# Layer 1's node stage: own values and residual added by TensorE, the result taken out by ScalarE

## The reference, cut to what matters

```
q = ((src @ q_w.T + q_b) * scaling).reshape(n, H, HD)
...
ex = jnp.exp(w - mx[e_dst])
den = jax.ops.segment_sum(ex, e_dst, num_segments=n)
attn_w = ex / (den[e_dst] + 1e-16)
msgs = attn_w[:, :, None] * v[e_src]
agg = jax.ops.segment_sum(msgs, e_dst, num_segments=n)
attn_out = agg.reshape(n, D) @ out_w.T + out_b
x = _batchnorm(src + attn_out, g1, b1)
ff = jax.nn.leaky_relu(x @ lin1_w.T + lin1_b, negative_slope=0.01)
ff = ff @ lin2_w.T + lin2_b
x = _batchnorm(x + ff, g2, b2)
```

## Time and profile before

| | |
|---|---|
| median of 3 runs | 5938.26 us (5937.13 to 5941.97) |
| profiled execution | 5949.69 us |
| its span | 5947.6 us |
| busy over the span | PE 70%, DVE 64%, ACT 32%, POOL 68% |
| mean granted TensorE clock | 0.756 |
| node stage, from L2335 to the first product of the feed-forward part | 2352.6 to 2402.7 us |

### The profile page before, as it was taken

The page is one execution under the profiler, slowest core; times in us unless marked ns, Lnnn a source line. Parts: engine busy times, 40 slices in busy tenths (PEclk is TensorE's granted clock), DMA queues, the critical chain, the costliest instruction groups (busy, mean ns, idle before and its releaser), DMA issues. The chain is left out here.

```text
span 5947.6 us, 86128 instructions
## 1 busy us (share of the span) xinstructions
PE 4163.2 (70%) x19030; PEld 3346.8 (56%) x19030; DVE 3780.3 (64%) x11775; ACT 1879.7 (32%) x4142; POOL 4018.2 (68%) x4191
## 2 busy tenths in 40 slices
PE   4788888867777676897788788444444457777776
PEld 4677776746666565444555555333333346666665
DVE  8565555547777777646666666444444447777776
ACT  5132222233343332463333333011111123444443
POOL 2677777757777775006777777677777767777773
PEclk9988778767777876998888888655555557777777
DMA  2554444434444444165554554222222234545442
GB/s 59 132 140 117 120 117 120 119 109 136 140 136 136 140 136 123 59 288 171 157 159 154 161 155 153 65 64 68 63 69 64 69 111 137 151 144 149 147 147 78
DMA packets 426775, 738.45 MB, mean 124 GB/s; under 512 B 100522, under 2 KB 280579, under 8 KB 419700
## 3 DMA queue, kind: packets, MB, share of 16 engines
q0 software_dynamic: 173200, 436.47, 26.2%
q1 hardware_dynamic: 244484, 289.62, 14.7%
q10 hardware_dynamic: 8592, 6.82, 0.4%
HBM read 613.55 MB, written 120.20 MB: 123 GB/s over the span
## 5 line engine op out<-in xcount | busy, mean ns | idle before, releaser
L1629 POOL DMA_INDIRECT xh<-pair_d,src_i x1658 | 1587.8, 958 | 558.0 <-issue 490.4
L2660 POOL DMA_INDIRECT l2e_rows<-msg_d,msg_i x829 | 790.0, 953 | 567.8 <-POOLq L61 315.4
L855 POOL DMA_INDIRECT l2f_rows<-msg_d,msg_i x829 | 786.7, 949 | 280.3 <-issue 242.4
L1000 POOL DMA_INDIRECT l0e_rows<-node_d,src_i x829 | 790.5, 954 | 260.4 <-issue 227.2
L1157 PE MATMUL l0e_ps<-l0e_rows,l0e_sel 128*128 128x256 f32 x1664 | 715.1, 522 | 189.0 <-DVE early_acc L1224 79.9
L889 PE MATMUL l2f_ps<-l2f_rows,l2f_sel 128*128 128x128 f32 x1664 | 426.3, 422 | 571.4 <-DVE l2f_sel L908 355.0
L889 PEld LDWEIGHTS l2f_ps<-l2f_rows,l2f_sel 128*128 128x128 f32 x1664 | 371.8, 315 | 653.3 <-DVE l2f_sel L908 387.5
L2794 PE MATMUL l2e_ps<-l2e_rows,l2e_sel 128*128 128x256 f32 x1664 | 544.0, 458 | 77.6 <-DVE l2e_sel L2886 40.4
L1224 DVE TENSOR_TENSOR early_acc<-early_acc,l0e_ps 128x264 f32 x832 | 356.5, 429 | 338.4 <-PE l0e_ps L1158 267.0
L920 DVE TENSOR_TENSOR xh<-xh,l2f_ps 128x128 f32 x832 | 238.9, 287 | 509.7 <-PE l2f_ps L889 402.8
L2851 DVE TENSOR_TENSOR l_acc<-l_acc,l2e_ps 128x256 f32 x832 | 349.3, 420 | 312.5 <-PE l2e_ps L2794 307.0
(11 more groups left out here) (465 smaller groups left out, 8347.7 us busy)
## 6 DMA issues: line engine op xcount, KB each, us to landing
l0e_rows<-in_edge_attr_dram SPq DMA_DIRECT2D x832, 64.0 KB
msg_d<-l1t_queries SPq DMA_DIRECT2D x50, 1024.0 KB, 3.9
l1te_local<-local_d SPq DMA_DIRECT2D x52, 512.0 KB
l2e_local<-local_d SPq DMA_DIRECT2D x52, 512.0 KB
l3te_local<-local_d SPq DMA_DIRECT2D x52, 512.0 KB
xh<-pair_d,src_i POOLq DMA_INDIRECT x1658, 2.8
msg_d<-l2e_msg SPq DMA_DIRECT2D x50, 512.0 KB
l0e_rows<-node_d,src_i POOLq DMA_INDIRECT x829
```

What stands on the lines that cost most here:

```text
L855: pool.indirect_dma_start(rows[:, t % R, :], None, table, bass.IndirectOffsetOnAxis(index[:, t:t + 1], 0)) \
L1000: pool.indirect_dma_start(rows[:, t % R, 0:D], None, table, bass.IndirectOffsetOnAxis(g.src_i[:, t:t + 1], 0)).then_inc(gathered[t % R], 16)
L1629: pool.indirect_dma_start(rows[:, t % R, :], None, g.pair_d, bass.IndirectOffsetOnAxis(g.src_i[:, t:t + 1], 0)).then_inc(gathered[n % RG], 16)
L2660: pool.indirect_dma_start(rows[:, t % R, :], None, table, bass.IndirectOffsetOnAxis(index[:, t:t + 1], 0)).then_inc(gathered[t % R], 16)
```

## The change

Three things move. VectorE's `add_own` is gone: in `turn` TensorE makes for each window two products with the identity, one of the scaled sums and one of the weighted own values, both into the same PSUM range, so that their sum comes out transposed. VectorE's `leave` is gone: in `mix` TensorE adds a product of the identity with the residual in `yt` to the output product, and ScalarE writes `yt` from PSUM with the bias (Identity). VectorE keeps scale_sum, which now sets `summed`, and count. The waits go along: TensorE now waits for `weighted` and for `h_in`, ScalarE for `ob_in` and `mixed`.

```
+                        act.wait_ge(ob_in, 32)
+                        for k in range(NG + 1):
+                            if k < NG:
+                                act.wait_ge(turned, k + 1)
+                                if k >= 2:
+                                    act.wait_ge(mixed, k - 1)
+                                nc.scalar.copy(zt[:, k % 2, 0:cols(k)[1]], pt[k % 2][:, 0:cols(k)[1]]).then_inc(moved, 1)
+                            if k >= 1:
+                                act.wait_ge(mixed, k)
+                                nc.scalar.activation(yt[:, cols(k - 1)[0]], po[(k - 1) % 2][:, 0:cols(k - 1)[1]], ACT.Identity,
+                                                     bias=ob[:, 0:1]).then_inc(taken, 1)
...
                         def turn(k):
                             lo, hi = of_group(k)
                             pe.wait_ge(summed, k + 1)
+                            pe.wait_ge(weighted, k + 1)
                             if k >= 2:
                                 pe.wait_ge(moved, k - 1)
                             for j in range(hi - lo):
-                                mm = nc.tensor.transpose(pt[k % 2][:, j * D:(j + 1) * D], acc3[:, lo + j, 0:D], g.ident[:, :])
+                                one = pt[k % 2][:, j * D:(j + 1) * D]
+                                nc.tensor.matmul(one, acc3[:, lo + j, 0:D], g.ident[:, :], start=True, stop=False)
+                                mm = nc.tensor.matmul(one, v3[:, lo + j, :], g.ident[:, :], start=False, stop=True)
                             mm.then_inc(turned, 1)
...
+                            pe.wait_ge(h_in[part_of(k)], 16)
+                            nc.tensor.matmul(po[k % 2][:, 0:cols(k)[1]], g.ident[:, :], yt[:, cols(k)[0]], start=True, stop=False)
                             nc.tensor.matmul(po[k % 2][:, 0:cols(k)[1]], ow[:, :], zt[:, k % 2, 0:cols(k)[1]],
-                                             start=True, stop=True).then_inc(mixed, 1)
+                                             start=False, stop=True).then_inc(mixed, 1)
...
                         def scale_sum(k):
                             lo, hi = of_group(k)
                             nc.vector.tensor_tensor(by_head(acc3, lo, hi), by_head(acc3, lo, hi), per_head(top, lo, hi),
-                                                    ALU.mult).then_inc(dv, 1)
...
-                            nc.vector.tensor_tensor(acc3[:, lo:hi, 0:D], acc3[:, lo:hi, 0:D], v3[:, lo:hi, :],
-                                                    ALU.add).then_inc(summed, 1)
...
-                            nc.vector.scalar_tensor_tensor(yt[:, cols(k)[0]], po[k % 2][:, 0:cols(k)[1]], ob[:, 0:1],
-                                                           yt[:, cols(k)[0]], ALU.add, ALU.add).then_inc(taken, 1)
+                                                    ALU.mult).then_inc(summed, 1)
```

## The result

The changed kernel takes 5951.85 us (median of 18 runs, 5945.77 to 5956.48), the kernel before in the same rounds 5940.23 (18 runs): ratio 1.0018, 95% interval 1.0011 to 1.0024, which is 6.5 to 14.3 us more, 10.7 in the middle; the two medians lie 11.6 us apart. I predicted +10.9 us and gave 0.62 to less than 0.2%; the interval reaches over 0.2%, so on which side the change lies isn't settled. The median itself, 5951.85 for 5949.2, has the drift of the medians of before in it (5938.26, then 5940.23). One of the 11 executions of a later version, the kernel before with TensorE kept busy ahead of the feed-forward part, took 7722.0 us and is left out of its ratio.

A forecast was written before the change was run, and what follows sets the result against it. No single engine bounds the run; VectorE paces this stage, TensorE would after the change. TensorE ends at 2362.2 + 43.8 + 2.8 = 2408.8 against 2397.92, +10.9 us: median 5949.2 us, range 5945 to 5954.5.

The forecast's parts named there:

- VectorE paces before, TensorE after: Changed stage after the softmax factors: VectorE, busy 40.36 of 41.00 us, loses 21.0 us; TensorE becomes the bound at 43.8.
- A group costs 3.50 us: TensorE per full group: eight identity products, 1.79 us, plus four wide records, 1.71 us; 12.5 groups make 43.8 us.
- The four-pass estimate: Alternative TensorE price from four passes per float32 product: 3.41 us a group, 42.7 in all, time 5948.1 us.
- The start comes 2.9 us earlier: TensorE's first product follows the first scaling, at 2362.2 instead of 2365.13, a gain of 2.9 us.
- The clock takes 2.8 us at the start: TensorE's first 5.6 us in the stage run at half clock, losing 2.8 us; bounds 0 to 6.8 us low.
- The tail keeps its 4.8 us: From TensorE's last product of the stage to the feed-forward part: unchanged at 4.8 us.
- ScalarE's output costs what its copy does: ScalarE's 13 new outputs from PSUM cost the copies' 0.57 us each, 1.2 us a group together.
- Rival (c): TensorE enters the feed-forward part at full clock, saving 2.8 us there: +8.1 us, 5946.4; chance 0.12.
- the two clock terms: TensorE's low clock at the stage's start and at the feed-forward part's start, each taken to lose 2.8 us.

The follow-up runs named there:

- the own-value half: Kernel before, with own values added by TensorE's identity products, output and residual left to VectorE: 5938.28 against 5940.69 us, ratio 0.9996.
- the version without own values: Changed kernel with the product adding the own values left out, one identity product per window: groups 35.32 us in its profile, no run time given.
- the version with two groups: Changed kernel, own values by TensorE for two groups only, then VectorE; TensorE kept busy in both idle times: 5944.65 against before's 5950.14 us, ratio 0.9991.

## Why the prediction was right

*VectorE paces before, TensorE after.* Right: 23.97 of 41.00 us busy became 42.00 of 42.00.

*A group costs 3.50 us.* Right to the second decimal, by the period after, by 43.90 us for 12.5 groups at full clock, and by the 2.61 with one product less. Both source rows held: the pair elsewhere in the program for the narrow ones and the feed-forward part's rate for the wide ones. The four-pass estimate (3.41 a group) was the less exact of the two.

*The start comes 2.9 us earlier.* Right: 1.48 us after the first scaling for 4.41.

*The clock takes 2.8 us at the start.* Too large for this execution: 3.2 us at the lower level, 1.6 lost, which is 45.41 for the groups where the sum had 46.6. The size lies inside the bounds that I gave (0 to 6.8 us low). It isn't a constant: the own-value half and the version without own values, which start as densely, had 5.6 and 5.4 us.

*The tail keeps its 4.8 us.* Right: 4.74 for 4.76.

*ScalarE's output costs what its copy does.* Wrong, 0.69 us for 0.59 at 512 columns, and without effect, as 0.69 more per group had none either.

*Rival (c)*, the feed-forward part entered at full clock, was half there: the clock was up at its first product and fell 0.8 us later, so M is 87.9 for 89.0. In the profile of before it had fallen at 2401.48 (0.74 in the mean of 2401 to 2402), ahead of the first product. The reason that the rival gives, that TensorE was dense until shortly before, isn't shown: in the own-value half TensorE was as dense (32.40 of 32.40 us), and its clock had fallen at 2395.3 (0.65 in the mean of 2395 to 2396), ahead of the first product at 2396.13, with M 89.3. In the profiled execution the two clock terms together take 2.3 us off my sum, L + M is +8.6 and not +10.9; the 18 runs, each with its own clock history, have +10.7. I can't say from them whether the mean clock loss is nearer to my 2.8 us, since the interval is some 8 us wide. That 10.7 lies so near to 10.9 is in part luck.

The reason that the change loses although it takes 21.0 us off VectorE is thus shown from both sides: TensorE had 17 us of slack in this stage, either half of the change uses most of it, and the second half is paid for: on top of the own values, the residual makes the groups 45.41 us instead of 35.84, 9.6 more, for 10.7 by the sum less 1.2 of a shorter low stretch.

## What to carry to other kernels

When work is moved from the engine that paces to one with slack, price the receiver's whole group at its own rates first, and compare that with the present period; here 3.50 us stood against the present 32.8 / 12.5 = 2.6. Moving one half was free and moving both was not, so move piece by piece until the two loads meet. In a stage of some 40 us the matrix engine's clock at its start is a term of its own, and filling its idle time ahead with products that nobody needs gave 1.5 us here and 2.7 in the next part, in one profiled execution each; neither alone shows in the time of the runs.

## What was not expected of the hardware

An Identity with a bias from PSUM over 512 columns took ScalarE 0.69 us, a copy of the same range 0.59. TensorE's clock was at full in the first 0.8 us of the feed-forward part after, although TensorE had stood idle 3.70 us ahead of it, and fell only then; in the version with two groups it fell in the same way about a microsecond into dense work, after 2.0 us idle. So the level at the first instruction says little about the next microseconds. And a VectorE operation of two SBUF inputs beside GpSimd mostly took 1.54 us and alone 0.67 to 0.68, which made the same addition worth moving in the first groups and not in the later ones.
